# A fused attention and feed-forward layer on one core, without the constant products in its first three steps

## The reference

```
q = layernorm(x) @ Wq;  k, v = split(ctx @ Wkv)
q, k = rope(q, pos), rope(k, pos)
w = softmax(q k^T / sqrt(8))              (per head, 128 x 128)
x = x + (w v) @ Wout + bout
xq = clip(round(layernorm(x) / s1), -8, 7)
h  = relu(xq @ W1q^T + b1q);  hq = clip(round(h / s2), 0, 15)
x = x + hq @ W2q^T * scale + b2q
```

## Time and profile before

| | |
|---|---|
| median of 3 runs | 249.44 us |
| all runs | 249.44, 250.34, 249.37 us |
| the profiled execution | 249.89 us, of which 248.0 us are the span of the profile |
| mean granted TensorE clock | 0.962 |
| PE busy | 221.0 us (89%), 3222 instructions |
| DVE, ACT, POOL busy | 196.6, 185.6, 140.5 us (79%, 75%, 57%) |

### The profile page before, as it was taken

One profiled execution on the slowest core, in us unless ns is written; L12 is line 12 of the kernel. 1 busy time (PEld: TensorE's weight loads), 2 busy tenths in 40 slices (PEclk: granted clock), 3 DMA queues, 4 the chain that ended last, 5 costly groups with the idle time before them and its releaser, 6 DMA issues.

```text
span 248.0 us, 8414 instructions
## 1 busy us (share of the span) xinstructions
PE 221.0 (89%) x3222; PEld 175.7 (71%) x3222; DVE 196.6 (79%) x418; ACT 185.6 (75%) x346; POOL 140.5 (57%) x232
## 2 busy tenths in 40 slices
PE   1649985888999999999999999999999999999753
PEld 1448873767688888888888888888787877677531
DVE  6869578858797979797989898989898887884641
ACT  1402468477779797979797979797979798888662
POOL 1678466494948484848484848484846470421220
PEclk9968998699999999999999999999999999999995
DMA  7596005700000001000100010001000100010101
GB/s 147 217 335 231 5 0 163 268 4 1 5 4 4 4 1 46 5 5 5 44 4 4 4 48 1 5 4 46 4 5 1 49 4 5 11 40 1 46 0 42
DMA packets 11382, 11.30 MB, mean 46 GB/s; under 512 B 3920, under 2 KB 10576, under 8 KB 11216
## 3 DMA queue, kind: packets, MB, share of 16 engines
q1 hardware_dynamic: 8864, 10.23, 12.6%
q10 hardware_dynamic: 2480, 0.54, 1.1%
HBM read 8.41 MB, written 2.10 MB: 42 GB/s over the span
## 4 chain that ended last, share of the span: by engine, by line
PE 71%; POOL 7%; issue 7%; DVE 6%; ACT 5%; DMA 2%; ACTq 1%; POOLq 0%; DVEq 0%
PE ps_misc L951 43%; PE ps_av L951 13%; PE ps_exp L951 12%; PE ps_max L951 3%; DVE mx L801 3%; ACT h_i L608 2%; DMA wkv<-in_L_xattn_Wkv_dram 2%; POOL rot L446 2%; POOL xcT_hi L433 1%; ACT qk_rows L552 1%; POOL v_strip L397 1%; ACT w_i L618 1%; POOL xcT_lo L436 1%; DVE by_cos L791 1%; POOL qk_rows L457 1%
## 5 line engine op out<-in xcount | busy, mean ns | idle before, releaser
L801 DVE TENSOR_REDUCE mx<-ps_max 128x8 f32<-128x1024 f32 x64 | 77.9, 1218 | 10.6 <-PE ps_max L951 10.5
L578 ACT ACTIVATE expo<-ps_exp 128x1024 f32<-128x1024 f32 x64 | 67.3, 1052 | 7.7 <-PE ps_exp L951 7.5
L446 POOL TENSOR_TENSOR rot<-by_cos,by_sin 128x256 f32<-128x256 f32 x32 | 23.1, 743 | 54.0 <-DVE by_sin L791 54.0
L608 ACT ACTIVATE h_i<-ps_misc,b1q,relu_scale 128x128 int16<-128x128 f32 x128 | 48.8, 486 | 1.0 <-PE ps_misc L951 1.0
L951 PE MATMUL ps_exp<-q_stack,k_stack 25*128 25x128 f32 x512 | 42.9, 284 | 4.6 <-DVE mx L801 2.4
L951 PEld LDWEIGHTS ps_exp<-q_stack,k_stack 25*128 25x128 f32 x512 | 34.4, 187 | 16.5 <-DVE mx L801 8.5
L951 PE MATMUL ps_misc<-ident,qk_rows 128*128 128x128 f32 x256 | 41.6, 287 | 1.8 <-POOL qk_rows L457 0.8
L951 PE MATMUL ps_av<-expo,v_strip 128*32 128x128 f32 x1024 | 41.0, 279 | 0.0
L951 PEld LDWEIGHTS ps_misc<-ident,qk_rows 128*128 128x128 f32 x256 | 28.3, 143 | 7.2 <-issue 2.8
L951 PEld LDWEIGHTS ps_av<-expo,v_strip 128*32 128x32 f32 x1024 | 24.1, 109 | 9.1 <-issue 5.9
L565 ACT CAST q_stack<-ps_misc 128x512 fp32r<-128x512 f32 x32 | 19.8, 623 | 13.1 <-PE ps_misc L951 13.1
(11 more groups left out here) (119 smaller groups left out, 455.4 us busy)
## 6 DMA issues: line engine op xcount, KB each, us to landing
w<-in_L_ffn_W_dram SPq DMA_DIRECT2D x2, 1024.0 KB, 6.3
out_dram<-y SPq DMA_DIRECT2D x8, 256.0 KB, 2.1
xcT<-in_ctx_dram SPq DMA_DIRECT2D x1, 1536.0 KB, 7.7
x_all<-in_x_dram SPq DMA_DIRECT2D x1, 1024.0 KB, 10.1
xcT<-in_ctx_dram SPq DMA_DIRECT2D x1, 768.0 KB, 7.2
x_all<-in_x_dram SPq DMA_DIRECT2D x1, 512.0 KB, 8.1
q_stack<-mxT SPq DMA_DIRECT2D x32, 8.0 KB
xcT<-in_ctx_dram SPq DMA_DIRECT2D x2, 192.0 KB, 4.2
```

The source lines that it names most:

```text
L446: pool.tensor_tensor(out[:, :, c, :], kept[:, :, c, :], turned[:, :, 1 - c, :], ALU.add).then_inc(rot_ready, 1)
L578: act.activation(expo[:, at, :], ps_exp[:, :, :].rearrange("p m t -> p (m t)"), ACT.Exp, scale=SCALE)\
L608: ins = act.activation(h_i[:, r, f, :], ps_misc[PIECE_BANK[(H0, H1)[half]]][:, 128 * c:128 * c + 128], ACT.Relu, bias=b1q[:, f:f + 1], sca ...
L801: dve.tensor_reduce(out=mx[:, r, 8 * unit:8 * unit + 8], in_=ps_max[:, :, :].rearrange("p m (i k) -> p (m i) k", i=4), axis=AX.X, op=ALU.m ...
```

## The change

`keep_busy` and its twelve calls are taken out. The order of all that remains, its waits and all other engines are as before. The diff, its first and last parts in full and the middle cut:

```diff
@@ -994,13 +994,6 @@
-            def keep_busy(n):
-
-                pe.wait_ge(id_ready, 4)
-                pe.wait_ge(ident_bf_ready, 1)
-                for _ in range(n):
-                    mm(ps_av[:, 0:256], ident_bf[:, :], ident[:, :].bitcast(BF16))
-
@@ -1181,32 +1174,18 @@
             def body(st):
                 late = Step(st.s - 1)
-                if st.s == 1:
-                    keep_busy(8)
-                if late.s == 0:
-                    keep_busy(8)
                 if late.has(S_MAX):
                     transpose_maxima(late, 0, S_MAX, MX0)
                 if st.s == 2:
                     transpose_weight_maxima()
                 if late.has(S_ATT):
                     weigh_values(late, 1)
-                if st.s == 2:
-                    keep_busy(8)
-                if st.s == 0:
-                    keep_busy(8)
...
                 if late.has(S_PROJ):
                     project_v(late)
-                if st.s == 1:
-                    keep_busy(8)
-                if st.s == 0:
-                    keep_busy(8)
-                if st.s == 1:
-                    keep_busy(8)
...
```

## The result

The changed kernel takes 252.54 us (median of 6 runs, 251.86 to 253.51) against 249.67 us for the kernel before (median of 6, 249.0 to 250.34): a ratio of 1.0106, 95% interval 1.0082 to 1.0130. It is slower by 2.9 us. The profiled execution took 251.90 us, 2.01 over the profiled one of before. All ratios in this document leave out executions that took over 1.5% more than the fastest one of the same kernel (none of these twelve did), while the medians take in all.

A forecast was written before the change was run, and what follows sets the result against it. The prediction took TensorE (71% of the chain of waits) as the bound, hardly waiting from about 44 us. Step 1's +0.77 and step 2's +1.75 gave +2.52 on the 249.44 median: 252.0 us, range 250.0 to 253.5.

The forecast's parts named there:

- Step 0, 0: 16 removed products ahead of the real product at 15.53, which waits for the last weight part: worth 0.
- The queue gives back 0.70: Batch 0's query transposes, held behind 40 removed products, start at 23.21 instead of 23.91: 0.70 us won.
- Four transposes, +0.51: Batch 0's query transposes until ACT can copy them: 1.15 us at 1.2 GHz for 0.64 at 2.4.
- Step 1's projection, +0.96: Query and key projection, first product to by_cos of batch 1: 2.32 us at 1.2 GHz for 1.36.
- Net of step 1, +0.77: Queue gain of 0.70 against slower transposes (+0.51) and slower projection (+0.96) before by_cos of batch 1.
- Step 2, +1.75: Low clock from the transposes at 31.91: +0.79 from first transpose to first projection product, +0.96 for the projection.
- The rest of step 2 and the chain to 44, 0: Last two removed groups gain nothing; the chain over GpSimd, ACT and DVE to 44.02 carries the delay one to one.
- The low stretch after 44, 0: Low clock from TensorE's step at 44.02 assumed as long as before, 4.1 us: 0, possibly -0.7 to +1.1.
- From 60 us on nothing may differ but the offset: In the profile after, everything from 60 us on is only shifted by the delay from the fill.
- Rival 1: Real work brings the clock back, full at step 2's projection; only +0.77 is left: 250.2 us; chance 0.20.
- Rival 2: The low clock after 44 us lasts longer, adding 1.1 us: 253.1 us; chance 0.14.
- Rival 3: The queue counts and the clock does not: 0.70 won, 248.7 us; chance 0.10, including no effect at all.

## Why the prediction was right, and where its terms were not

The time (252.0 forecast, +2.52 on the median then shown; 252.54 and +2.87 measured), the sign and the mechanism held: the removed products were worth the clock of the work behind them. But the sum was better than its terms, and that is in part luck: in step 1 a credit and a price that were both too large took each other away, and the excess of step 2's term stands against a loss in the runs that no profile explains.

- *Step 0, 0:* right by the runs (ratio 0.9992). The profile shows 0.19 us that I had excluded with "the work of 15.53 waits for GpSimd".
- *The queue gives back 0.70:* mis-sized. In the kernel before the hold was 0.70 in the one profile that I had; in others of kernels with the same groups it was 0.00, 0.01, 0.01, 0.19 and 1.06. So the credit was nearer 0.3 than 0.7.
- *Four transposes, +0.51:* 24.62 - 23.50 = 1.12 for the 1.15 forecast. Right.
- *Step 1's projection, +0.96:* 27.14 - 25.26 = 1.88 for 2.32, because the clock rose near 26.4, in its middle; in the second profile 27.41 - 25.34 = 2.07. Too large by 0.25 to 0.44. In the kernel with step 2's products alone the clock did not rise in it, and it took 27.49 - 25.16 = 2.33, as priced.
- *Net of step 1, +0.77:* by the profiles about right. From the first projection product to by_cos of batch 1 it takes 10.65 us on average in the six kernels with step 1's groups whole (10.32 to 11.37), and 11.50 in the four without them (11.28 to 11.73): 0.85 us, and 0.19 more for the late first product. The runs say more: the kernel without the products of steps 0 and 1 lost 1.9 us by its ratio. Some 0.8 us of that no profile explains.
- *Step 2, +1.75:* the term that was most too large. The kernel without its products lost 1.0, and from by_cos of batch 1 to by_cos of batch 2 the changed kernel took 36.55 - 27.14 = 9.41 us for 8.03, so 1.38 more (1.25 in its second profile). The price of the projection was right (36.55 - 34.25 = 2.30 for 2.32), the time from the first transpose to it too large (34.25 - 32.50 = 1.75 for 2.10), since the clock fell only at 33.3, behind the first transposes. The step's term took the low clock as given from its start; it is a matter of where the fall lies, and the runs average over that.
- *The rest of step 2 and the chain to 44, 0:* right. 1.97 us of delay at by_cos is 1.96 at step 3's start.
- *The low stretch after 44, 0:* right in its length. It lasted 50.3 - 45.98 = 4.3 us, for 4.1. But the delay did not pass it whole: the DMA of the maxima, which the kernel before waits for longer, took 0.36 us off it.
- *"From 60 us on nothing may differ but the offset":* true to 240 us, where the offset is 1.61. The clock's earlier fall in the drain made it 2.02. The prediction looked for moves of the clock in the fill only.

Rival 1 (the real work holds the clock) is refuted by the row that I had named: the clock was 0.50 at step 2's projection in both profiles of the changed kernel. Ahead of that fall TensorE had been busy for 3.24 of 6.70 us, close to the 3.35 of 6.90 that I had counted. The rule of the Trainium skill that there be no long idle gaps between bursts ("TensorE: Matmul & The Clock Gate", section "Why this matters for your kernels") was not enough to hold the clock here: the longest idle time ahead of the fall was 2.89 us, and the kernel before had fallen with 1.11 us of idle in all. Rival 2 did not come about: the low stretch after step 3's start lasted 4.3 and 4.7 us in the two profiles. Rival 3 falls with the sign. The wait for the DMA of the maxima I had overlooked, though it stands in the kernel before with 0.83 us; in the kernel with more products it decided.

## What to carry to other kernels

Constant products in an engine's idle time are worth what the clock takes from the work behind them: price that work at both clock levels from the profile, and take off what the products hold up. The moments at which the clock moves differ from one execution to the next, so a hold or a rise read from one profile is a draw, not a term; run the halves apart, and look at every single execution beside the ratio. Before keeping the clock up in a new place, see what ends the next wait: an engine that is faster only up to a late DMA waits, and may pay for that with its clock. And where a view names what ended a wait, look in the program whether the work reads it.

## What was unexpected of the hardware

- Constant transposes raised and held TensorE's clock as well as constant products did, each among the same real work (ratio 0.9999, 192 of them for 96 products).
- After a wait of 2.66 us the clock fell and stayed at 0.50 for over 13 us of nearly unbroken work (50.8 to 64.0), and the kernel lost 5.1 us.
- The clock also falls in the drain, at moments that differ from profile to profile, and one way there takes 3.44 us behind the fall and 3.03 ahead of it.
- After 8.6 to 8.9 us of idle time TensorE's first product started 0.25 us behind its data, after 4.9 to 6.4 us 0.05 to 0.06 us.
- Ahead of the clock's first recorded change the profile reads 1.00, also where products take 0.41 us as they do at 1.2 GHz.
